# Message passing as matrix products: the order of high and low parts within a block of sources

## The chip, the cores and the metric

The kernel runs on one core of a Trainium2 chip. The metric is the device time of one execution in microseconds. The kernel before takes 4105.4 us, the median of three runs (4103.71 to 4105.85).

## The reference, cut to what matters

A graph of 6250 nodes with 128 features and 100,000 edges goes through four graph networks with a layer norm and a residual around each. Every layer sums, for each node, rows of its neighbours:

```python
agg = jax.ops.segment_sum(h[src], dst, num_segments=N)
```

This sum is needed three times in the first network (GIN: two dense layers with batch norm follow each time), once in the second (with a sigmoid gate per edge, then a GRU cell), five times in the third (a matrix product before the sum, a GRU cell after it) and once in the fourth (one matrix product after it). The edges are the same in all of them.

## The kernel before, in words

The kernel first sorts the edges and builds a matrix of counts: for each pair of nodes, how many edges go from the one to the other, one byte each, kept in DRAM. Nodes are padded to 49 blocks of 128 (`NB = 49`). A segment sum is then a dense product of the features with the count matrix. Counts are small integers; features are float32.

TensorE's one-pass float32 format (fp32r) does not keep all bits of a float32. So each 128x128 block of features is split in two: `high` (VectorE, L2540, the upper bits), copied to `hi` by ScalarE (L2402), and `lo`, the rest, by GpSimd (L2127). Both are multiplied with the same counts and added up in the same PSUM bank. This pair of products is L2188, the line of the change.

The targets are cut into three thirds (`THIRDS`), since PSUM holds only a part of all sums. For one third, TensorE goes through all 49 blocks of sources (`k` = 0 to 48) and adds each block's products up in four or five banks. These are the chunks of `SUMS`: third 0 has five chunks (384, 512, 512, 512, 512 columns), third 1 four of 512, third 2 four (512, 512, 512, 256). A block of sources of one third is called a source here; it is numbered `g` over the whole flow, and `g // 49` tells the part, a layer and a third of it. `k == 0` starts each bank anew, `k == NB - 1` ends it and tells the engines that take the sums out (`summed`, and `used` for the last chunk).

For each source, a DMA on SyncE's queue (L2073) brings a row of counts as bytes into a ring. ScalarE widens the first 1024 or 768 columns to fp32r (`wide_act`), VectorE the rest (`wide_dve`), both at L2036. There are three slots for widened rows and for `hi` and `lo`; `used`, which goes up with the last matmul of a source, frees them. Before a source's first matmul TensorE waits for `hi`, `lo` and `wide_act`; before the first chunk that goes beyond ScalarE's columns it waits for `wide_dve`.

The order of work on TensorE is written out by a loop over steps `g` (L2151). After each source it issues whatever of the layer behind is due at that step: products of the GRU cell (L2306 to L2309), dense layers (L2314, L2323), transposes (L2350) and others, each a few short matmuls in F32. `LAG`, `EVERY`, `LEAVE`, `ENTER` and `CHAIN` hold the distances in steps. There are two flows: the first with the three sums of the first network (one third of the first is made earlier, at L643) and the gated sum, the second with the five of the third network and the last one. The gated sum does not go by L2188: its counts are weighed by gates first (`weighing`), and its products are L2184, chunk after chunk with the same stationary block in plain F32. All others, 26 parts of 49 sources, go by L2188: nine of third 0, eight of third 1, nine of third 2.

Of the kernel before, what the change touches and what calls it, by code (L numbers as in the profile page):

```python
# [25 lines left out]
NB = -(-N // P)  # L26
# [32 lines left out]
SUMS = [[(128, 384), (512, 512), (1024, 512), (1536, 512), (2048, 512)],  # L59
        [(0, 512), (512, 512), (1024, 512), (1536, 512)],  # L60
        [(0, 512), (512, 512), (1024, 512), (1536, 256)]]
# [4 lines left out]
WIDE_SLOTS = 3  # L66
CUT_SLOTS = 3
# [1802 lines left out]
class Flow:  # L1870
# [95 lines left out]
    def run(self):  # L1966
        net, nc, ps = self.net, self.net.nc, self.net.ps
# [16 lines left out]
        with ExitStack() as tmp, stage(nc, *names) as (block, s):  # L1984
            wide = scratch(nc, tmp, "wide", [P, WIDE_SLOTS, ROW_BYTES], F32R)
            high = scratch(nc, tmp, "high", [P, CUT_SLOTS, P], I32)
            hi = scratch(nc, tmp, "hi", [P, CUT_SLOTS, P], F32R)
            lo = scratch(nc, tmp, "lo", [P, CUT_SLOTS, P], F32R)
# [11 lines left out]
            if self.enter is not None:  # L2000
                c0, size = row_slots * ROW_BYTES, self.enter.steps * 3 * D * 4
# [32 lines left out]
            def widen(copy, g, c0, c1):  # L2034
# [4 lines left out]
            whole, rest = (final[0:FULL_P * NB, :].rearrange("(p k) f -> p (k f)", k=NB),  # L2039
                           final[FULL_P * NB:N, :].rearrange("(a k) f -> a (k f)", a=1)) if final is not None else (None, None)  # L2040
# [105 lines left out]
            def _(e):  # L2146
                if self.enter is not None:
                    for n in range(self.enter.steps):
                        ins = e.transpose(ps[:, 2 + n // 4, n % 4 * D:(n % 4 + 1) * D], self.enter.weights[:, n, :], net.ident[:, :])
                    ins.then_inc(s["w_turned"], 1)  # L2150
                for g in self.steps:  # L2151
                    for n in combined_at(g):
                        e.wait_ge(s["w_cut"], 2)
                        for i in range(3):
                            ins = e.matmul(ps[:, n, i * D:(i + 1) * D], turned_w[:, n * D:(n + 1) * D], self.enter.w_in[i], start=True, stop=True)  # L2155
                        ins.then_inc(s["w_made"], 1)
                    if 0 <= g < total:
                        n, q, k = self.where(g)
                        weighing = g >= plain
                        if weighing:  # L2160
                            e.wait_ge(s["lv_sent"], self.need[n][k])
                        else:
                            e.wait_ge(s["hi"], g + 1)
                            e.wait_ge(s["lo"], g + 1)
                            e.wait_ge(s["wide_act"], g + 1)
                        early = not weighing
                        for c, (w0, size) in enumerate(SUMS[q]):
                            if early and w0 + size > BY_ACT[q]:
                                e.wait_ge(s["wide_dve"], g + 1)
                                early = False  # L2170
                            if weighing:
                                e.wait_ge(s["weighed"], self.weighed_upto(g, c))
                            if weighing and k == 0 and c == 4:
                                e.wait_ge(s["lv_relu"], len(leaves))
                                e.wait_ge(s["lv_scored"], len(leaves))
                            if self.enter is not None and g == 0:
                                e.wait_ge(s["w_kept"], self.enter.steps)
                            if k == 0 and g:
                                dve, act = self.taken(g // NB - 1, c + 1)
                                e.wait_ge(s["took_dve"], dve)  # L2180
                                if act:
                                    e.wait_ge(s["took_act"], act)
                            if weighing:
                                ins = e.matmul(ps[:, c, 0:size], source(n, k), weights(g, c), start=k == 0, stop=k == NB - 1,  # L2184
                                               skip_group_check=True)
                                ins.then_inc(s["attended"], 1)
                            for part in () if weighing else (hi, lo):
                                ins = e.matmul(ps[:, c, 0:size], part[:, g % CUT_SLOTS, :], wide[:, g % WIDE_SLOTS, w0:w0 + size],  # L2188
                                               start=k == 0 and part is hi, stop=k == NB - 1 and part is lo,
                                               skip_group_check=True)  # L2190
                            if not weighing and k == NB - 1 and c + 1 < len(SUMS[q]):
                                ins.then_inc(s["summed"], 1)
                        if not weighing:
                            ins.then_inc(s["used"], 1)

                    for c in self.entering_at(g - ENTER["turned"]):
# [5 lines left out]
                        for b in range(c.blocks):  # L2202
                            ins = e.transpose(ps[:, 5, b * P:(b + 1) * P], room[0][c.made % 2][:, b * P:(b + 1) * P], net.ident[:, :])  # L2203
                        ins.then_inc(s["turned"], 1)
                    for c in self.entering_at(g - ENTER["back"]):
# [4 lines left out]
                        for b in range(c.blocks):  # L2210
                            ins = e.transpose(ps[:, 5, PAIR + b * P:PAIR + (b + 1) * P], room[1][c.made % 2][:, b * P:(b + 1) * P],  # L2211
                                              net.ident[:, :])
# [36 lines left out]
                    for c in self.due(g - LEAVE["turned"], "leave"):  # L2249
# [5 lines left out]
                        for b in range(c.blocks):  # L2255
                            ins = e.transpose(ps[:, 6, b * P:(b + 1) * P], room[2][c.late % 2][:, b * P:(b + 1) * P], net.ident[:, :])
# [598 lines left out]
```

## Time and profile before

| | |
|---|---|
| median of three runs | 4105.4 us |
| span of the profiled execution | 4103.4 us |
| TensorE matmuls busy | 3757.5 us, 92% |
| TensorE weight loads busy | 2938.1 us, 72% |
| VectorE / ScalarE / GpSimd busy | 75% / 61% / 33% |
| matmuls at L2188 | 11074 |
| share of L2188 in the chain that ended last | 40% of the span |

The profile is of one execution; its span runs from the first instruction to the last, and no other time of that execution is given. PE is TensorE's matmuls, PEld its weight loads, DVE VectorE, ACT ScalarE, POOL GpSimd, SP SyncE. Matmuls overlap, so the duration of one is not what it costs; the distance between two starts in the timeline is. Starts are shown to 0.01 us.

### The profile page before, as it was taken

Reading aid. Unit: us, or ns where it says so; the run is one execution under the profiler, and the core shown is the slowest. Engines: PE = TensorE matmul, PEld = TensorE weight load, DVE = VectorE, ACT = ScalarE, POOL = GpSimd, SP = SyncE. Lnnn points to the kernel's source line nnn. Section 1 sums busy time; section 2 is a strip of 40 time slices with the busy share of each in tenths; the row PEclk is TensorE's granted clock in tenths of the full one; section 3 lists DMA queues with packets and bytes.
Section 4 is the critical chain, followed back from the end, with each engine's and each line's share of the span. In section 5 each row is a group of like instructions: output and inputs, shape, how many; then the busy total and the mean of one; then the engine's idle time right before and its main releaser. Section 6 shows DMA issues by size and latency. Waiting matters only on the chain.

```text
span 4103.4 us, 59929 instructions
## 1 busy us (share of the span) xinstructions
PE 3757.5 (92%) x17331; PEld 2938.1 (72%) x17331; DVE 3059.9 (75%) x5526; ACT 2493.7 (61%) x4754; POOL 1354.9 (33%) x1941
## 2 busy tenths in 40 slices
PE   0128899999999999999899999999999999999999
PEld 0116678888888644555688888888888888888887
DVE  9989956576587777878668667766866876786685
ACT  1119956656656787777565655565565565566655
POOL 0021135533545310000361343244244234346624
PEclk9999999999999999999999999999999999999999
DMA  2019964544543322221143344344344434433444
GB/s 63 0 56 363 366 197 124 141 130 124 144 130 105 93 70 77 71 63 54 58 113 108 107 128 119 107 126 125 108 121 123 110 104 129 121 100 110 117 133 135
DMA packets 234209, 489.81 MB, mean 119 GB/s; under 512 B 32580, under 2 KB 100925, under 8 KB 233496
## 3 DMA queue, kind: packets, MB, share of 16 engines
q1 hardware_dynamic: 213084, 432.93, 37.0%
q0 software_dynamic: 7856, 46.93, 3.2%
q10 hardware_dynamic: 12938, 6.05, 0.7%
q8 instruction: 146, 2.39, 0.3%
q14 instruction: 185, 1.51, 0.1%
HBM read 396.99 MB, written 43.87 MB: 107 GB/s over the span
## 4 chain that ended last, share of the span: by engine, by line
PE 50%; issue 0%; ACT 0%; DVE 0%; POOL 0%; ACTq 0%; POOLq 0%
PE ps L2188 40%; PE ps L2306 3%; PE ps L2307 3%; PE ps L2308 1%; PE ps L2309 1%; PE ps L2350 1%; PE ps L2336 0%; PE ps L2220 0%; PE ps L2292 0%; PE ps L2331 0%; PE ps L2226 0%; PE ps L2211 0%; ACT wide L2036 0%; PE ps L2203 0%; PE ps L2155 0%
## 5 line engine op out<-in xcount | busy, mean ns | idle before, releaser
L2188 PE MATMUL ps<-wide,hi 128*128 128x512 f32 (+2 forms) x5537 | 2135.8, 388 | 19.1 <-issue 9.5
L2188 PE MATMUL ps<-wide,lo 128*128 128x512 f32 (+2 forms) x5537 | 2075.4, 379 | 0.0
L2036 DVE CAST wide<-ring 128x1536 fp32r<-128x1536 uint8 (+2 forms) x1274 | 1311.7, 1030 | 551.0 <-PE ps L2188 546.5
L2188 PEld LDWEIGHTS ps<-wide,hi 128*128 128x128 f32 x5537 | 1041.1, 188 | 221.3 <-issue 29.5
L2188 PEld LDWEIGHTS ps<-wide,lo 128*128 128x128 f32 x5537 | 1042.8, 188 | 185.7
L2036 ACT CAST wide<-ring 128x768 fp32r<-128x768 uint8 (+1 forms) x1274 | 1153.0, 905 | 3.2 <-DMA ring<-count 2.3
L2402 ACT CAST hi<-high 128x128 fp32r<-128x128 f32 x1274 | 381.6, 299 | 983.8 <-PE ps L2188 605.2
L2127 POOL TENSOR_TENSOR lo<-hN,high 128x128 fp32r<-128x128 f32 x686 | 566.6, 829 | 761.5 <-PE ps L2188 468.5
L2127 POOL TENSOR_TENSOR lo<-hB,high 128x128 fp32r<-128x128 f32 x588 | 500.4, 852 | 763.2 <-PE ps L2188 545.6
L2184 PE MATMUL ps<-hN,hB 128*128 128x512 f32 (+1 forms) x1274 | 525.1, 569 | 5.6 <-DVE aggT L2365 4.2
L2395 ACT ACTIVATE hN<-aggT,source_scores 128x512 f32<-128x512 f32 (+1 forms) x637 | 428.7, 695 | 118.0 <-PE ps L2184 86.7
L2531 DVE TENSOR_TENSOR hN<-hN,ring 128x512 f32<-128x512 f32 (+1 forms) x637 | 402.8, 668 | 108.8 <-ACT hN L2395 103.7
L2184 PEld LDWEIGHTS ps<-hN,hB 128*128 128x128 f32 x1274 | 241.1, 191 | 263.5 <-issue 208.8
L2556 DVE SCALAR_TENSOR_TENSOR room<-ps,b2h,room 128x256 f32<-128x256 f32 (+1 forms) x125 | 59.8, 479 | 245.4 <-ACT room L2423 245.4
L2540 DVE TENSOR_SCALAR high<-hN 128x128 int32<-128x128 int32 x686 | 234.7, 342 | 8.9 <-DVE hB L2648 4.2
L2540 DVE TENSOR_SCALAR high<-hB 128x128 int32<-128x128 int32 x588 | 204.6, 348 | 0.6 <-POOL lo L2127 0.6
L679 ACT ACTIVATE aggT<-ps 128x1024 uint16<-128x1024 f32 x196 | 165.6, 846 | 26.3 <-PE ps L629 26.2
L475 PE MATMUL ps<-ident,aggT 128*128 128x128 f32 x112 | 27.6, 427 | 166.3 <-DVE aggT L184 166.3
L2423 ACT ACTIVATE room<-ps,b2s 128x256 f32<-128x256 f32 (+1 forms) x250 | 103.9, 467 | 119.7 <-PE ps L2309 118.6
L2307 PE MATMUL ps<-hT,wT 128*128 128x256 f32 (+1 forms) x600 | 175.8, 375 | 0.0
L629 PEld LDWEIGHTS ps<-right,left 128*128 128x128 bf16 x1225 | 99.2, 158 | 97.5 <-DVE left L586 46.7
L2090 POOL TENSOR_SCALAR states_bn<-states_bn 128x1 f32<-128x1 f32 x1 | 0.2, 231 | 506.6 <-POOLq L144 506.6
(246 smaller groups left out, 3477.1 us busy)
## 6 DMA issues: line engine op xcount, KB each, us to landing
ring<-count SPq DMA_DIRECT2D x490, 320.0 KB, 2.9
ring<-count SPq DMA_DIRECT2D x441, 256.0 KB, 2.6
ring<-count SPq DMA_DIRECT2D x490, 224.0 KB, 2.5
wide<-aggT POOLq DMA_DIRECT2D x49, 896.0 KB, 6.1
count<-aggT SPq DMA_DIRECT2D x49, 800.0 KB, 4.0
xN<-in_x ACTq DMA_DIRECT2D x1, 2744.0 KB
out<-xN SPq DMA_DIRECT2D x1, 1064.0 KB
out<-xN SPq DMA_DIRECT2D x1, 896.0 KB
```

Of the source, the lines that this page charges most:

```text
L679: e.activation(rows[k % ROW_BUFFERS][:, t0 * P:t1 * P], ps[:, bank:bank + 2, :].rearrange("p b f -> p (b f)") [:, 0:(t1 - t0) * P], ACT.Co ...
L2036: return copy(wide[:, g % WIDE_SLOTS, c0:c1].rearrange("p (t u f) -> p t u f", u=2, f=P), rows[:, g % row_slots, c0:c1].rearrange("p (t f ...
L2127: e.tensor_tensor(lo[:, g % CUT_SLOTS, :], source(n, k), high[:, g % CUT_SLOTS, :].bitcast(F32), ALU.subtract)\
L2184: ins = e.matmul(ps[:, c, 0:size], source(n, k), weights(g, c), start=k == 0, stop=k == NB - 1, skip_group_check=True)
L2188: ins = e.matmul(ps[:, c, 0:size], part[:, g % CUT_SLOTS, :], wide[:, g % WIDE_SLOTS, w0:w0 + size], start=k == 0 and part is hi, stop=k = ...
L2306: e.matmul(o, gates_of(c)[g_], net.aggT[:, c.cols], start=True, stop=False)
L2307: e.matmul(o, gru.w_state[g_], net.hT[:, c.cols], start=False, stop=True)
L2395: e.activation(weights(g, c), layers[n].target_scores[:, sums_at(q, c)], ACT.Sigmoid, bias=layers[n].source_scores[:, k:k + 1]).then_inc(s ...
L2402: e.copy(hi[:, g % CUT_SLOTS, :], high[:, g % CUT_SLOTS, :].bitcast(F32)).then_inc(s["hi"], 1)
L2423: e.activation(room[i][u][:, 0:c.size], ps[:, bank, i * PAIR:i * PAIR + c.size], ACT.Sigmoid, bias=self.step(c).b_sum[i]).then_inc(s["rz"], 1)
L2531: e.tensor_tensor(gate, gate, rows[:, g % row_slots, c0:c1].rearrange("p (t f u) -> p t u f", u=2, f=P), ALU.mult).then_inc(s["weighed"], 1)
L2540: e.tensor_scalar(high[:, g % CUT_SLOTS, :], source(n, k).bitcast(I32), HIGH_BITS, None, ALU.bitwise_and)\
```

## The change

For the sources `0 < k < NB - 1` of the parts that aren't weighed, the loop over the chunks issues only the product with `hi`; a second loop over the chunks then issues the products with `lo`. Before, each chunk got `hi` and then `lo`. The waits keep their place ahead of the chunks of the first loop, and `used` goes up with the last matmul of the second. The first and the last source of each part keep the old order, as do the products at L643 and L2184.

```diff
--- before.py
+++ after.py
@@ -2164,6 +2164,7 @@
                             e.wait_ge(s["lo"], g + 1)
                             e.wait_ge(s["wide_act"], g + 1)
                         early = not weighing
+                        whole = not weighing and 0 < k < NB - 1
                         for c, (w0, size) in enumerate(SUMS[q]):
                             if early and w0 + size > BY_ACT[q]:
                                 e.wait_ge(s["wide_dve"], g + 1)
@@ -2184,12 +2185,15 @@
                                 ins = e.matmul(ps[:, c, 0:size], source(n, k), weights(g, c), start=k == 0, stop=k == NB - 1,
                                                skip_group_check=True)
                                 ins.then_inc(s["attended"], 1)
-                            for part in () if weighing else (hi, lo):
+                            for part in () if weighing else (hi,) if whole else (hi, lo):
                                 ins = e.matmul(ps[:, c, 0:size], part[:, g % CUT_SLOTS, :], wide[:, g % WIDE_SLOTS, w0:w0 + size],
                                                start=k == 0 and part is hi, stop=k == NB - 1 and part is lo,
                                                skip_group_check=True)
                             if not weighing and k == NB - 1 and c + 1 < len(SUMS[q]):
                                 ins.then_inc(s["summed"], 1)
+                        for c, (w0, size) in enumerate(SUMS[q]) if whole else ():
+                            ins = e.matmul(ps[:, c, 0:size], lo[:, g % CUT_SLOTS, :], wide[:, g % WIDE_SLOTS, w0:w0 + size],
+                                           start=False, stop=False, skip_group_check=True)
                         if not weighing:
                             ins.then_inc(s["used"], 1)
 
```

## Rows read from the trace of the kernel before

**Rows 1.** The page: its first line, TensorE's busy time, and its granted clock in 40 slices.

```profile
span 4103.4 us, 59929 instructions
...
PE 3757.5 (92%) x17331; PEld 2938.1 (72%) x17331; DVE 3059.9 (75%) x5526; ACT 2493.7 (61%) x4754; POOL 1354.9 (33%) x1941
...
PEclk9999999999999999999999999999999999999999
```

**Rows 2.** The page, chain that ended last, shares of the span by line.

```profile
PE ps L2188 40%; PE ps L2306 3%; PE ps L2307 3%; PE ps L2308 1%; PE ps L2309 1%; PE ps L2350 1%; PE ps L2336 0%; PE ps L2220 0%; PE ps L2292 0%; PE ps L2331 0%; PE ps L2226 0%; PE ps L2211 0%; ACT wide L2036 0%; PE ps L2203 0%; PE ps L2155 0%
```

**Rows 3.** Groups of instructions: form, count, busy us, mean ns, idle before.

```profile
L2188 PE MATMUL ps<-wide,hi 128*128 128x512 f32 (+2 forms) x5537 | 2135.8, 388 | 19.1 <-issue 9.5 <-ACT wide L2036 5.7 <-ACT aggT L2367 1.5
L2188 PE MATMUL ps<-wide,lo 128*128 128x512 f32 (+2 forms) x5537 | 2075.4, 379 | 0.0
...
L2188 PEld LDWEIGHTS ps<-wide,lo 128*128 128x128 f32 x5537 | 1042.8, 188 | 185.7
...
L2184 PE MATMUL ps<-hN,hB 128*128 128x512 f32 (+1 forms) x1274 | 525.1, 569 | 5.6 <-DVE aggT L2365 4.2 <-DVE aggT L2369 1.4
...
L2184 PEld LDWEIGHTS ps<-hN,hB 128*128 128x128 f32 x1274 | 241.1, 191 | 263.5 <-issue 208.8 <-DVE hN L2531 38.3
```

**Rows 4.** One stretch: us, busy (x instructions) by engine, clock, DMA share, GB/s.

```profile
2400.00:2900.00 500.00, 499.43 (x2340) 421.37 (x2339) 355.65 (x603) 291.20 (x566) 184.54 (x209) 1.00 0.43 118
```

**Rows 5.** Line L2036 alone: who waited for it (us, times).

```profile
  PE ps L2188: 5.7, 1
```

**Rows 6.** Timeline at 1176 us: start, duration, engine, line, operation; VectorE, then TensorE.

```profile
1174.32 1.48 DVE L2036 CAST wide<-ring 128x1280 fp32r<-128x1280 uint8 x1
...
1176.59 0.40 PE L2188 MATMUL ps<-wide,lo 128*128 128x512 f32 x1
```

**Rows 7.** Timeline of TensorE, third 1; 16 matmuls of L2188 between these.

```profile
2582.73 0.39 PE L2188 MATMUL ps<-wide,hi 128*128 128x512 f32 x1
...
2586.58 0.39 PE L2188 MATMUL ps<-wide,lo 128*128 128x512 f32 x1
```

**Rows 8.** Timeline of TensorE, third 0, one source to the next.

```profile
2423.06 0.34 PE L2188 MATMUL ps<-wide,lo 128*128 128x384 f32 x1
2423.24 0.40 PE L2188 MATMUL ps<-wide,hi 128*128 128x512 f32 x1
...
2424.39 0.39 PE L2188 MATMUL ps<-wide,lo 128*128 128x512 f32 x1
...
2425.24 0.34 PE L2188 MATMUL ps<-wide,lo 128*128 128x384 f32 x1
```

**Rows 9.** Timeline of TensorE, third 2; the last row is eight sources later.

```profile
2707.14 0.28 PE L2188 MATMUL ps<-wide,lo 128*128 128x256 f32 x1
2707.26 0.40 PE L2188 MATMUL ps<-wide,hi 128*128 128x512 f32 x1
...
2720.10 0.28 PE L2188 MATMUL ps<-wide,lo 128*128 128x256 f32 x1
```

**Rows 10.** Timeline of TensorE, third 1, after two transposes; ten steps.

```profile
2589.40 0.38 PE L2350 MATMUL ps<-ident,hT 128*128 128x128 f32 x2
...
2589.85 0.39 PE L2188 MATMUL ps<-wide,lo 128*128 128x512 f32 x1
...
2592.16 0.39 PE L2188 MATMUL ps<-wide,lo 128*128 128x512 f32 x1
```

**Rows 11.** Timeline of TensorE, third 1, after one transpose; eight steps.

```profile
3209.70 0.27 PE L2350 MATMUL ps<-ident,hT 128*128 128x128 f32 x1
...
3210.05 0.39 PE L2188 MATMUL ps<-wide,lo 128*128 128x512 f32 x1
...
3211.87 0.39 PE L2188 MATMUL ps<-wide,lo 128*128 128x512 f32 x1
```

**Rows 12.** Timeline of TensorE: F32 passes, first and sixth row (x2: two passes).

```profile
2427.25 0.59 PE L2306 MATMUL ps<-aggT,ring 128*128 128x256 f32 x2
...
2429.41 0.59 PE L2309 MATMUL ps<-aggT,ring 128*128 128x256 f32 x2
```

## The prediction

> **What bounds the kernel now.** I read the page first. TensorE is busy for 3757.5 of 4103.4 us at the full granted clock, 2.4 GHz [rows 1], and the chain that ended last gives 40% of the span to L2188 alone [rows 2]. In a 500 us window of the second flow PE is busy for 499.43 us at clock 1.00 [rows 4]: here the time is what TensorE needs to get through its list. The groups of instructions [rows 3] then give the list: L2188 issues 5537 matmuls with the high part and as many with the low part, 11074 in all, and next to them just as many weight loads. The sum of the parts agrees: nine parts of third 0, eight of third 1 and nine of third 2, each with 49 sources at 10, 8 and 8 matmuls, are 4410 + 3136 + 3528 = 11074.
>
> The mean of 388 ns in that group is a latency, not a price, because matmuls overlap. The price is the distance from start to start in the timeline. In a quiet stretch of third 1, where all chunks have 512 columns, 17 starts take 2586.58 - 2582.73 = 3.85 us, 0.2265 us each [rows 7]. Within this stretch half of the steps go from the high to the low part of one chunk (same bank, same moving data, other weights) and half from the low part to the next chunk's high part (everything changes), and the pace does not tell them apart.
>
> **What the change touches.** For 47 of 49 sources of each part (k = 0 and k = 48 stay) 11074 x 47/49 = 10622 matmuls are put in another order. None is added or removed. No instruction of another engine moves. The sum goes part by part:
>
> 1. Weight loads. After the change 4 of 5 (third 0) or 3 of 4 matmuls use the weights that the one before used. Does their load go away? The kernel has the same situation in L2184, where all chunks of a source are multiplied with one stationary block in a row: 637 products there are 1274 matmul passes with 1274 loads [rows 3]. So repeated weights are loaded again. These are F32 products of two passes each, so they don't prove it for the one-pass format of L2188, but they are the nearest rows. I take 11074 loads before and after. A load takes 188 ns and a matmul step 226.5, and PE's idle time before all of L2188's matmuls is 19.1 us, next to nothing of it for a load [rows 3]: loads lie under the matmul before. Kept or dropped, I cost them at 0; the end below zero, a stream that runs faster under unchanged weights, is rival C.
>
> 2. The wait for VectorE's half of the widened row. It now comes before the third matmul of a source instead of the fifth (third 0), and before the second instead of the third elsewhere: 0.45 or 0.23 us earlier. Queued behind it on PE is the whole rest of the source. In the whole trace PE waited for a widening once, for 5.7 us [rows 5], and the groups name ScalarE's half for it [rows 3]. The tightest place I found is at 1176 us: VectorE's cast starts at 1174.32 and takes 1.48, so it ends at 1175.80; the second matmul of that source, which will have the wait in front of it, starts at 1176.59 [rows 6]. That leaves 0.79 us. Cost 0; if this cover were gone, each source would lose at most the 0.23 or 0.45 us by which the wait is earlier, and none of them comes near.
>
> 3. Release of buffers and banks. The count that frees the widened row and the weight buffers still goes up with the last matmul of the source. Take-outs of the banks hang on k = 48, which keeps its order. The low part has been waited for at the source's start, as now. Cost 0.
>
> 4. The order of long and short matmuls. This is the only part for which the trace shows a price. A source of third 1 has equal chunks. A source of third 2 has 3584 columns over both parts, at 0.2265 us per 512 that is 1.585 us; eight sources in a row take 2720.10 - 2707.14 = 12.96 us, 1.620 each [rows 9]. So 35 ns are lost per source. Third 0 has 4864 columns, 2.152 us, and takes 2425.24 - 2423.06 = 2.18 [rows 8]: 28 ns lost. In third 1 nothing is lost, though the same conversions run beside it. What is different is the short chunk: 256 or 384 columns, twice in a row (high, low), after which the following 512s start 0.23 to 0.24 apart for a while (five steps from 2423.24 take 1.15 us, 1.132 at the steady pace) [rows 8]. Today these stretches cost 441 x (0.035 + 0.028) = 27.8 us, of which 423 x 0.063 = 26.6 lie in the reordered sources. After the change the two short matmuls of a source no longer stand together: each has three or four long ones behind it. So the cost lies between all of it gone (-26.6 us) and doubled (+26.6 us).
>
> To choose between the ends I looked at other short matmuls. After two 128-column transposes the ten steps from 2589.85 take 2.31 us, 45 ns over the steady 2.265 [rows 10]; after a single one the eight steps from 3210.05 take 1.82, 8 ns over 1.812 [rows 11]. That speaks for singles being cheaper than half a pair. Against it: within a pair the second short matmul is already late in giving way: 0.18 instead of 0.170 us for 384 columns [rows 8], 0.12 instead of 0.113 for 256 [rows 9]. So one short matmul before it is enough to start the loss, and after the change there would be two starts per source. I take the middle, 0. It is what one gets if the loss goes with the number of short matmuls, which doesn't change.
>
> Sum: 0 + 0 + 0 + 0 on 4103.4 us of span, which stands 2.0 us under the median of the runs, 4105.4. Forecast 4105 us.
>
> **Against a page.** The trace has one load per matmul, hidden, at 188 ns under a step of 226.5 [rows 3, 7]. The Trainium skill, "TensorE: Matmul & The Clock Gate", section "Step-by-step: what each phase is for", says that weights usually stay in the array over many matmuls, so that they are loaded once and used repeatedly; by that rule this order would be the better one. The same page under "Back-to-back issue gap" gives 512/2.4 + 2.5 = 216 ns for a 512-column step; the trace has 226.5 and the measurement decides. By the page the sum would gain some 10 ns on each step with unchanged weights, by the rows nothing.
>
> **Rivals.**
>
> A, slower: each short chunk restarts the slow stretch. The place is the step after each 256 or 384 column matmul of L2188. Full doubling is 26.6 us; in third 2 only three long matmuls follow a short one where six do now, so a stretch is cut in half, and third 0 sources near a gated chunk start in one anyway. Half the doubling, +13 us: 4118. It decides when a single short matmul is followed by more than half of today's loss.
>
> B, faster: a lone short matmul costs little, as after the lone transpose. Two singles are 16 of the 45 ns of a pair, so 64% of 26.6 us goes: -17 us, 4088. The two transposes are F32 and follow F32 products, which is what speaks against carrying their numbers over.
>
> C, faster by much: with unchanged weights the stream itself speeds up. What speaks for it: the nearest matmuls of about the same length, 256-column F32 passes, come every 2.16/10 = 0.216 us [rows 12], so 0.2265 is no floor. Of the 10622 matmuls, 423 x 8 + 376 x 6 + 423 x 6 = 8178 follow one with the same weights; at up to 10.5 ns that is 86 us: 4020. Against it: in those F32 passes the weights change each time, and the pace is as good, so weights are not what makes L2188 slower.
>
> D, slower: a step to another bank with the same weights, or the earlier wait, costs something that no row shows, 1 to 2 ns per matmul, 10 to 20 us: 4120.
>
> **How the numbers follow.** About 8 us, 0.2%, is what a measurement of this kernel can tell from no change. That is 0.8 ns per reordered matmul, so the middle is narrow. The forecast gets 0.45, with 4098 to 4112 as its own range: 0.39 of it within 0.2%, 0.03 on each side. A gets 0.24, B 0.20, C 0.07, D 0.04. Faster: 0.03 + 0.20 + 0.07 = 0.30. Same: 0.39. Slower: 0.03 + 0.24 + 0.04 = 0.31. The range from 4087 to 4121 holds the forecast, A, B and most of D, and leaves out C.
>
> **What would show it.** The page after should have 11074 loads at L2188 again; fewer would make step 1 wrong. A quiet stretch of third 1 should keep its 0.2265 us per matmul; if it gets shorter, C is right, if longer, D. The period of a third 2 source (1.620) and of a third 0 source (2.18) decide between the forecast, A and B: 20 to 30 ns up is A, as much down is B. A new wait of PE for VectorE's L2036 would make step 2 wrong. My prediction is wrong if the period of any of the three kinds moves by more than 15 ns.

## The result and the profile after

The changed kernel takes 4112.45 us (median of 16 runs, 4109.90 to 4113.42). The kernel before, run in turn with it on the same chip, takes 4104.97 us (16 runs, 4102.96 to 4106.57). The ratio is 1.0017, 95% interval 1.0010 to 1.0024: slower by 7.5 us. That is a hair under the 8 us that the prediction set as the bound of "no change", but the interval of this comparison leaves no change out, and 4112.45 lies above the forecast's own range of 4098 to 4112 and inside the wide one. The mechanism was forecast at zero, and it is not zero.

The page after: first line, busy times, granted clock, and the chain by line. It answers to [rows 1, 2].

```profile
span 4111.7 us, 59929 instructions
...
PE 3766.1 (92%) x17331; PEld 2938.1 (71%) x17331; DVE 3060.2 (74%) x5526; ACT 2493.8 (61%) x4754; POOL 1353.0 (33%) x1941
...
PEclk9999999999999999999999999999999999999999
...
PE ps L2189 21%; PE ps L2195 19%; PE ps L2310 3%; PE ps L2311 3%; PE ps L2313 1%; PE ps L2312 1%; PE ps L2354 1%; PE ps L2340 0%; PE ps L2224 0%; PE ps L2296 0%; PE ps L2335 0%; PE ps L2230 0%; PE ps L2215 0%; ACT wide L2036 0%; PE ps L2207 0%
```

This profiled execution took 4113.42 us, span 4111.7: 8.3 us over the span of before. The same 17331 matmuls and as many loads are there, PE is busy 8.6 us longer, and VectorE and ScalarE do what they did. L2188 has become L2189 (all high parts, and both parts at k = 0 and 48) and L2195 (the low parts); their shares of the chain, 21 and 19%, are the 40% of before. The time is in PE's stream itself. The two lines by form, as in [rows 3], and, from line L2036 alone, who waited for it, as in [rows 5]:

```profile
L2189 PE MATMUL ps<-wide,hi 128*128 128x512 f32 (+2 forms) x5537 | 1490.1, 389 | 19.0 <-issue 9.5 <-ACT wide L2036 5.7 <-ACT aggT L2371 1.5
L2195 PE MATMUL ps<-wide,lo 128*128 128x512 f32 (+2 forms) x5311 | 1348.5, 379 | 0.0
...
L2189 PEld LDWEIGHTS ps<-wide,hi 128*128 128x128 f32 x5537 | 995.6, 188 | 210.9 <-issue 29.6 <-DVE aggT L2369 2.6 <-ACT hi L2406 1.8
L2195 PEld LDWEIGHTS ps<-wide,lo 128*128 128x128 f32 x5311 | 961.0, 188 | 189.7
...
L2189 PEld LDWEIGHTS ps<-wide,lo 128*128 128x128 f32 x226 | 43.2, 191 | 6.9
```

```profile
  PE ps L2189: 5.7, 1
```

5537 + 5311 + 226 = 11074 loads, as before: repeated weights are loaded again. Idle time ahead of the matmuls stays at 19.0 us, and the one wait for a widening is still the 5.7 us one. (The busy column can't be held against before: matmuls of one line that follow each other overlap, and now four or five do, so the overlaps count once.)

**Where the time is.** First the steady pace. In the timeline x4 or x5 means that many matmuls in one row. After, TensorE in a quiet stretch of third 1, two sources and a half, up to the products of the GRU cell:

```profile
2586.28 1.07 PE L2195 MATMUL ps<-wide,lo 128*128 128x512 f32 x4
2587.18 1.07 PE L2189 MATMUL ps<-wide,hi 128*128 128x512 f32 x4
...
2589.90 1.07 PE L2195 MATMUL ps<-wide,lo 128*128 128x512 f32 x4
2590.81 0.59 PE L2310 MATMUL ps<-aggT,ring 128*128 128x256 f32 x2
```

20 steps take 4.53 us, 0.2265 each, exactly [rows 7]. Then the starts of four parts in a row, after and before: third 0, third 1, third 2, the next third 0.

```profile
2726.54 0.41 PE L2189 MATMUL ps<-wide,hi 128*128 128x384 f32 x1 [0.30 <-ACT aggT L2371]
...
2854.01 0.47 PE L2189 MATMUL ps<-wide,hi 128*128 128x512 f32 x1
...
2970.12 0.47 PE L2189 MATMUL ps<-wide,hi 128*128 128x512 f32 x1
...
3072.58 0.41 PE L2189 MATMUL ps<-wide,hi 128*128 128x384 f32 x1 [0.30 <-ACT aggT L2371]
```

```profile
2722.30 0.41 PE L2188 MATMUL ps<-wide,hi 128*128 128x384 f32 x1 [0.30 <-ACT aggT L2367]
...
2849.33 0.47 PE L2188 MATMUL ps<-wide,hi 128*128 128x512 f32 x1
...
2965.43 0.47 PE L2188 MATMUL ps<-wide,hi 128*128 128x512 f32 x1
...
3067.76 0.41 PE L2188 MATMUL ps<-wide,hi 128*128 128x384 f32 x1 [0.30 <-ACT aggT L2367]
```

Third 0 goes from 127.03 to 127.47 us, +0.44; third 1 from 116.10 to 116.11; third 2 from 102.33 to 102.46, +0.13. Over 47 sources that is 9 ns a source in third 0 and 3 in third 2 (other third 2 parts have +0.21: 4 to 5). A part's length is read to 0.01 us, a source's only to 10 ns, so the part is the better ruler. By it I took the difference of all 26 parts. All columns are in us against the profile of before. The last three are runs described below: after_again, third0_only and before_later4.

```
                                  after  same kernel  third 0  order of
                                         again        alone    before, 4 products ahead
third 0, first part               +0.67     +0.18      -0.05     -1.71
third 0, the other eight          +2.78     +2.93      +2.82     +0.09
third 1, all eight                +0.13     +0.18      +0.16     +0.16
third 2, seven parts              +1.03     +1.18      -0.05      0.00
third 2, gated part (1280-2020)   +1.79     +1.33      +1.32     +1.48
third 2, part with 3771           +1.73     +0.14      +1.49     -0.02
```

Two things are in this table. The order itself costs some 2.9 us in the eight later parts of third 0 and 1.1 in seven parts of third 2; the four traces of the changed kernel, as it is or with a few products added, agree within 0.3 us. And three single parts, the first and the last two of the table, move from trace to trace by up to 2 us, in kernels that have the old order there too. Those three are mainly the clock. Two windows, around the start of the gated sum and around 3771 us (us, busy by engine, granted clock, DMA share, GB/s), before and after:

```profile
1380.00:1400.00 20.00, 15.77 (x43) 8.22 (x42) 15.99 (x26) 15.97 (x25) 0.00 (x0) 0.91 0.27 68
3760.00:3790.00 30.00, 27.74 (x133) 23.23 (x133) 19.12 (x37) 18.22 (x35) 18.24 (x25) 1.00 0.52 144
```

```profile
1380.00:1400.00 20.00, 15.76 (x45) 8.69 (x44) 14.59 (x24) 14.85 (x22) 0.68 (x1) 0.83 0.28 80
3760.00:3790.00 30.00, 26.53 (x123) 21.62 (x122) 18.37 (x38) 18.35 (x37) 20.58 (x34) 0.94 0.50 136
```

The clock has two levels here, 2.4 and 1.2 GHz, and a stretch at 1.2 GHz counts half. So a mean of 0.91 over 20 us is about 3.6 us at half speed, 0.83 is 6.8 us, and 0.94 over 30 us is 3.6 us; half of each is lost. Before each stands an idle time of TensorE that both kernels have. The one ahead of the gated sum, before:

```profile
1387.16 5.23 PE L2184 MATMUL ps<-hN,hB 128*128 128x512 f32 x8 [4.24 <-DVE aggT L2365]
```

It is 4.24 us after the change too. The one ahead of 3771, before and after:

```profile
3767.27 0.47 PE L2188 MATMUL ps<-wide,hi 128*128 128x512 f32 x1 [1.96 <-issue]
```

```profile
3773.38 1.51 PE L2189 MATMUL ps<-wide,hi 128*128 128x512 f32 x4 [1.96 <-issue]
```

The idle time is 1.96 us in both, and only after is the clock halved behind it: four matmuls take 1.51 us where they take 1.07 elsewhere. None of this was in the prediction.

The third place is the start of the first flow. The clock is at half there in both kernels when the first part begins, and for how much longer differs from trace to trace. The first 10 us of that part in before, after, third1_only (old order in this part) and before_later4:

```profile
542.83:552.83 10.00, 10.00 (x37) 8.42 (x38) 5.88 (x9) 6.03 (x11) 5.34 (x5) 0.78 0.98 346
```

```profile
542.84:552.84 10.00, 10.00 (x35) 8.32 (x36) 5.35 (x9) 5.59 (x10) 4.81 (x5) 0.73 0.91 330
```

```profile
542.28:552.28 10.00, 10.00 (x35) 8.38 (x35) 5.25 (x9) 5.48 (x10) 4.06 (x5) 0.72 0.94 338
```

```profile
548.67:558.67 10.00, 10.00 (x46) 8.33 (x45) 4.09 (x6) 4.68 (x8) 3.72 (x3) 1.00 0.56 194
```

That is 2.2, 2.7, 2.8 and 0 us lost. It accounts for +0.5 of the +0.67 after, for the +0.52 of third1_only (which starts this part 0.55 us earlier, so that nothing is lost in all), and for the -1.71 in the last column of the table, whose first part begins behind the half clock. The order itself is left with about +0.2 in the first part.

The runs without a profile can't be sorted by what happened at 3771. The nine of the 16 with a mean clock of 0.993 or 0.994 have a median of 4112.8 us, the seven with 0.995 one of 4110.5, but the mean adds up all the falls of an execution. The profile of after_later1 (below) has the fall at 3771 and a mean of 0.995.

### The profile page after: what moved, and what is told of

Read it like the earlier page. It is cut to its first block, busy times and chain, and to the rows that moved or that the text cites. A ratio compares the mean times of both kernels' runs of the same rounds, so it can differ in the third digit from the quotient of the medians.

```text
span 4111.7 us, 59929 instructions
## 1 busy us (share of the span) xinstructions
PE 3766.1 (92%) x17331; PEld 2938.1 (71%) x17331; DVE 3060.2 (74%) x5526; ACT 2493.8 (61%) x4754; POOL 1353.0 (33%) x1941
## 4 chain that ended last, share of the span: by engine, by line
PE 50%; issue 0%; ACT 0%; DVE 0%; POOL 0%; ACTq 0%; POOLq 0%
PE ps L2189 21%; PE ps L2195 19%; PE ps L2310 3%; PE ps L2311 3%; PE ps L2313 1%; PE ps L2312 1%; PE ps L2354 1%; PE ps L2340 0%; PE ps L2224 0%; PE ps L2296 0%; PE ps L2335 0%; PE ps L2230 0%; PE ps L2215 0%; ACT wide L2036 0%; PE ps L2207 0%
## 5 line engine op out<-in xcount | busy, mean ns | idle before, releaser
L2036 DVE CAST wide<-ring 128x1536 fp32r<-128x1536 uint8 (+2 forms) x1274 | 1312.1, 1030 | 556.7 <-PE ps L2195 542.4
L2189 PE MATMUL ps<-wide,hi 128*128 128x512 f32 (+2 forms) x5537 | 1490.1, 389 | 19.0 <-issue 9.5
L2195 PE MATMUL ps<-wide,lo 128*128 128x512 f32 (+2 forms) x5311 | 1348.5, 379 | 0.0
L2036 ACT CAST wide<-ring 128x768 fp32r<-128x768 uint8 (+1 forms) x1274 | 1153.2, 905 | 3.2 <-DMA ring<-count 2.3
L2189 PEld LDWEIGHTS ps<-wide,hi 128*128 128x128 f32 x5537 | 995.6, 188 | 210.9 <-issue 29.6
L2195 PEld LDWEIGHTS ps<-wide,lo 128*128 128x128 f32 x5311 | 961.0, 188 | 189.7
L679 ACT ACTIVATE aggT<-ps 128x1024 uint16<-128x1024 f32 x196 | 165.6, 846 | 26.6 <-PE ps L629 26.5
```

What stands on the lines that cost most here:

```text
L679: e.activation(rows[k % ROW_BUFFERS][:, t0 * P:t1 * P], ps[:, bank:bank + 2, :].rearrange("p b f -> p (b f)") [:, 0:(t1 - t0) * P], ACT.Co ...
L2036: return copy(wide[:, g % WIDE_SLOTS, c0:c1].rearrange("p (t u f) -> p t u f", u=2, f=P), rows[:, g % row_slots, c0:c1].rearrange("p (t f ...
L2195: ins = e.matmul(ps[:, c, 0:size], lo[:, g % CUT_SLOTS, :], wide[:, g % WIDE_SLOTS, w0:w0 + size], start=False, stop=False, skip_group_che ...
```

## The experiments

Each kernel ran on a chip together with the kernel before, and its ratio is to that. The medians of before: 4105.42 for third1_only, shorts_together and the two equal ones; 4104.87 for third0_only, mirror, four_shorts and before_later; 4105.48 for before_later6, before_later4, after_later1 and after_again; 4105.71 for the two filled ones. A ratio of 11 runs carries an interval of about 0.0009, or 3.7 us, to each side, so kernels 1 to 2 us apart are told apart by the parts of their profiles and not by these medians. "Quiet part" means a part of third 0 and of third 2 in the stretch of the rows above, in the second flow (127.03 and 102.33 us before).

**third1_only: the new order only where all chunks are equal.** It has the repeated weights, the steps to another bank and the earlier wait, without short chunks.

```
-  whole = not weighing and 0 < k < NB - 1
+  whole = not weighing and 0 < k < NB - 1 and q == 1
```

> The new order only in third 1, where all chunks have 512 columns. Theory (slow stretches after short chunks): the matmul step stays 0.2265 us, the eight third 1 parts take the same 860.3 us from their second to their last source, time within 1 us of the kernel before. Rival (the weights that stay, the change of bank or the earlier wait for VectorE cost something per matmul): third 1 gets longer by its share of the change, some 2 to 3 of the 7.5 us. Second rival (half-clock spells come more often in the new order, wherever it is): more than 3.4 us of spells beyond those of the kernel before.

4105.39 against 4105.42 us, ratio 0.9999 [0.9990, 1.0008]; the eight third 1 parts together +0.03 us. So repeated weights gain nothing, and the other bank and the earlier wait cost nothing there: rivals C and D fall. The Trainium skill, "TensorE: Matmul & The Clock Gate", section "Step-by-step: what each phase is for", has weights loaded once and used repeatedly; here this order has the load each time and no gain, and the measurement decides.

**third0_only: the counterpart.** The same line with `and q == 0`.

> The new order only in third 0. From the trace of the changed kernel, third 0 as a whole is 3.5 us longer and third 2 1.0 us without its two clock spells. Theory: this kernel takes 3.5 us more than before plus what clock spells it gets, 4109. Rival (all of the change comes from clock spells): 4105 to 4107, with third 0 as before.

4110.39 us, 1.0013 [1.0004, 1.0022]. The starts of third 0, third 1, third 2 and the next third 0 in it:

```profile
2725.10 0.41 PE L2189 MATMUL ps<-wide,hi 128*128 128x384 f32 x1 [0.30 <-ACT aggT L2371]
...
2852.55 0.47 PE L2189 MATMUL ps<-wide,hi 128*128 128x512 f32 x1
...
2968.66 0.47 PE L2189 MATMUL ps<-wide,hi 128*128 128x512 f32 x1
...
3070.97 0.41 PE L2189 MATMUL ps<-wide,hi 128*128 128x384 f32 x1 [0.30 <-ACT aggT L2371]
```

127.45 us (+0.42), 116.11, and 102.31, the old value. The loss of the quiet parts sits where the order is new. But its part with the gap at 3771 is longer by 1.49, with the old order in it and a mean clock of 0.94 in the same window as above: that part of the loss is not the order of that part's matmuls.

**shorts_together: the new order, third 0's short chunk last with the high part and first with the low part.** The two 384s of a source stand together again.

```
+  chunks = list(enumerate(SUMS[q]))
+  if whole and q == 0: chunks = chunks[1:] + chunks[:1]
   ... high part over chunks, low part over reversed(chunks)
```

> The new order, but each source's high loop ends with its short chunk and the low loop begins with it and goes through the chunks backwards, so that the two short matmuls stand together again, and weights still stay for 4 or 3 of the matmuls in a row. Theory: third 0 back to 2.18 us per source, third 2 to 1.62, total 4.5 us below the changed kernel (half-clock spells aside). Rival (unchanged weights or order of banks cost): as slow as the changed kernel, +0.17%.

4111.38 us, 1.0014 [1.0005, 1.0023]: 6.0 us over before, where I had expected some 3. The sequence of lengths is now exactly that of before (two shorts, then eight or six 512s), and only weights and banks follow each other differently. Starts of third 0 and third 1:

```profile
2726.90 0.41 PE L2192 MATMUL ps<-wide,hi 128*128 128x384 f32 x1 [0.32 <-ACT aggT L2374]
...
2854.06 0.47 PE L2192 MATMUL ps<-wide,hi 128*128 128x512 f32 x1
```

127.16 us, +0.13 where the new order has +0.44. In third 2 the reversal brings the two 256s together as well, and its quiet parts stay at +0.14 to +0.18, no less than after. So in the quiet parts splitting the pair costs 0.3 us of 0.44 in third 0 (7 ns a source) and nothing in third 2; the rest, 3 to 4 ns a source in both, is there with unchanged lengths. In the first flow the pair gains nothing: two parts of third 0 keep +0.28 to +0.30, as in after, and two parts of third 2 have +0.33, more than the +0.17 and +0.08 of after. Over the same eight and seven parts as in the table above the two thirds lose 1.9 and 1.3 us where after loses 2.8 and 1.0, so keeping the pairs together gives back some 0.6 of 3.8 us. Most of the loss is there although the lengths follow each other as before. It needs the short chunk all the same, since third1_only has none and costs nothing. The first part has +0.77, and both stretches of half clock are there (gated part +1.47, the part with 3771 +1.53).

**equal_before and equal_after: no short chunks at all**, third 0 as 4 x 486 + 488, third 2 as 4 x 448 columns, in the old and the new order.

```
+  PLAIN_SUMS = [[(128, 486), (614, 486), (1100, 486), (1586, 486), (2072, 488)],
+                SUMS[1], [(448 * c, 448) for c in range(4)]]
```

> The order of before, but the chunks of thirds 0 and 2 are of (nearly) one size: 486, 486, 486, 486, 488 and 4 x 448 columns instead of 384 + 4 x 512 and 3 x 512 + 256. Theory: no short chunk, no slow stretch: 2.152 us per source in third 0 instead of 2.180, 1.585 instead of 1.620 in third 2, 27 us less in all if 486 columns stream as well per column as 512: 4078 us. Rival (the loss belongs to the thirds' other work, not to the sizes): 4105 us.

> The same equal chunks with the new order. Theory: without short chunks the order costs nothing, so the same time as equal chunks in the old order, within 2 us. Rival (weights, banks or the wait): 7 us slower than that.

4117.80 us, 1.0029 [1.0018, 1.0041], and 4116.01 us, 1.0029 [1.0018, 1.0039]. The old order should have gained 27 us if short chunks were the whole cost. Its timeline, 14 steps of 448 columns:

```profile
2727.89 0.37 PE L2191 MATMUL ps<-wide,lo 128*128 128x448 f32 x1
...
2730.78 0.37 PE L2191 MATMUL ps<-wide,lo 128*128 128x448 f32 x1
```

2.89 / 14 = 0.206 us a step, where 448/512 of 0.2265 is 0.198. My 28 and 35 ns of "loss" per source were not only the price of a change of length: these sizes miss the steady pace even among themselves. (The chunks of 486 columns in third 0 also begin at other places of the widened row, which these two kernels don't separate from the size.) What the pair does settle is the order: with no shorts the new order is not slower than the old (a quiet third 0 part +0.78 against +1.13, third 2 +0.44 against +0.49 in most). The new order costs only where lengths differ.

**mirror: the old order, odd sources with their chunks backwards.** Four shorts meet, and there are half as many changes of length.

```
+  if not weighing and 0 < k < NB - 1 and k % 2:
+      chunks = chunks[::-1]
```

> The high and low products chunk by chunk as before, but every second source of a part goes through its chunks backwards, so that the short matmuls of two neighbouring sources stand four in a row and then 12 or 16 long ones. Theory 'per start' (each run of short matmuls costs one slow stretch, however many they are): the loss of 28 and 35 ns per source halves, 13 us less, 4092 us. Rival 'per short matmul' (the forecast's assumption): 4105 us, no change. Rival 'an order that differs costs by itself': above 4107.

4108.55 us, 1.0008 [0.9999, 1.0018]. The timeline where two shorts meet two:

```profile
2744.98 0.33 PE L2191 MATMUL ps<-wide,hi 128*128 128x384 f32 x1
2745.15 0.34 PE L2191 MATMUL ps<-wide,lo 128*128 128x384 f32 x1
2745.33 0.34 PE L2191 MATMUL ps<-wide,hi 128*128 128x384 f32 x1
2745.51 0.35 PE L2191 MATMUL ps<-wide,lo 128*128 128x384 f32 x1
2745.69 0.40 PE L2191 MATMUL ps<-wide,hi 128*128 128x512 f32 x1
```

Four shorts take 0.71 us, 0.68 at the steady pace. The quiet parts gain 0.12 (third 0) and 0.17 us (third 2), 3 to 4 ns a source, where a price per change of length gives 14 to 17 and a price per short matmul gives 0. So a fifth of the loss goes with the changes, and the rest is as good as untouched by halving them. Its part around 3771 is longer by 4.04 us: an idle time 18 us ahead of the gap grew from 1.41 to 2.61 us, and the clock fell there and behind the gap.

**four_shorts: the old order, two shorts instead of one** (448, 448, 512, 512, 512 and 512, 512, 384, 384), by the same table PLAIN_SUMS.

> The order of before with other chunk sizes: 448, 448, 512, 512, 512 in third 0 and 512, 512, 384, 384 in third 2, which makes four shorter matmuls in a row in each source. Theory 'per start': the loss per source stays about 28 and 35 ns, 4105 us. Rival 'per short matmul': it doubles, 4130 us. Rival 'sizes' (each chunk that isn't 512 columns costs by its own size, 448 some 5 ns over its share as with equal chunks): third 0 loses 20 ns from its four 448s and little else, 4100 to 4108.

4114.96 us, 1.0025 [1.0015, 1.0036], which is none of the three times expected; quiet parts +0.91 and +0.40, which is 19 and 9 ns a source, with as many changes of length as before: again neither 0 nor the doubling (28 and 35). But by equal_before a step of 448 among its like costs 8 ns over its share, so this number can't be divided further, and the kernel tells little.

**before_later, before_later6, before_later4: the old order, pushed later** by 7, 6 or 4 more F32 products of 512 columns ahead of the first source, to see whether the place in time alone brings the half clock.

```
+  if self.enter is None and g == 0:
+      for _ in range(DELAY):
+          e.matmul(ps[:, 0, 0:512], net.ident[:, :], net.hT[:, 0:512], start=True, stop=True)
```

> The kernel before, with seven extra F32 products of 512 columns (never read) ahead of the first source of the first flow, which move everything behind them about 6 us later. Theory 'place decides' (the changed kernel gets a half-clock spell at 3773 us because it arrives 6 us later at TensorE's idle gap of 2 us there): this kernel gets that spell too, in about as many runs as the changed one (granted clock 0.993 in half of them), and those are some 2 us above the rest: median 4112. Rival 'the order causes the spells': no spell, 4111 us in all runs, with clock 0.994 to 0.996.

> The kernel before with six extra F32 products ahead instead of seven, so everything behind comes 5.3 us later instead of 6.2. Theory 'position' (TensorE's 1.95 us gap near 3770 us is followed by a half-clock spell or not depending on where exactly it falls; 6.2 us later was a lucky place, 5.3 is not): this kernel gets the spell in most runs, granted clock 0.993 to 0.994, and is as slow as with seven products or slower although it is delayed less: 4111 to 4113. Rival 'the order of the products brings the spells on': no spell in the old order at any delay, 4110.3, clock 0.994 to 0.996.

> The same with four extra products, 3.6 us later. Theory 'position': no spell at the gap, as in the kernel before, 4108.5 us, clock 0.994 to 0.996. Rival 'any delay brings it': 4110.3 and clock 0.993.

4111.58, 4110.74 and 4108.99 us; 1.0017 [1.0008, 1.0026], 1.0013 [1.0004, 1.0022], 1.0009 [1.0000, 1.0018]. None has the half clock at 3771, though I had expected it of before_later and then of before_later6. before_later, with its gap ending 0.06 us from the place where it ends after the change:

```profile
3773.44 0.47 PE L2192 MATMUL ps<-wide,hi 128*128 128x512 f32 x1 [1.96 <-issue]
```

```profile
3760.00:3790.00 30.00, 26.54 (x130) 22.02 (x129) 19.15 (x40) 18.97 (x38) 21.23 (x34) 1.00 0.53 145
```

So "that place on the time axis" fell as the cause in its simple form. At the gated part they do tell something. before_later4 and before_later, the window 1380 to 1400:

```profile
1380.00:1400.00 20.00, 15.77 (x51) 9.71 (x50) 14.21 (x24) 14.44 (x23) 1.97 (x3) 0.83 0.31 90
```

```profile
1380.00:1400.00 20.00, 15.77 (x57) 10.27 (x56) 14.79 (x25) 15.04 (x24) 2.88 (x4) 0.91 0.38 103
```

The first has 0.83 and its gated part is longer by 1.48 us, the second 0.91 and +0.24: both have the order of before, so the order isn't needed for this difference. Over all traces, those with 0.91 have -0.08 to +0.71 us in this part and those with 0.83 have +1.10 to +2.20, with one exception (mirror: 0.83 and +0.54).

**after_later1 and after_again: the changed kernel with one such product, and unchanged once more.**

> The changed kernel with one extra F32 product of 512 columns ahead, 0.9 us more work. Theory 'position': most of its runs lose the spell, the group with clock 0.993 shrinks from half of the runs to a quarter or less, and the median falls or stays in spite of the extra work: 4111.4. Rival 'the order brings the spells on': 4113.3, half of the runs at 0.993.

> The changed kernel as it is, on the same chip as the three others, to compare with. All theories: 4112.4 us, two groups of runs, at 4110.5 and 4112.8; if the profiled run is one without the spell at 3773 us, its span is 1.7 us shorter than that of the first profile.

4111.22 us, 1.0014 [1.0005, 1.0023], and 4112.56 us (4109.54 to 4114.87), 1.0017 [1.0008, 1.0026]. The kernel with more work has the lower median, by 1.3 us, and 2 of 11 runs with a mean clock of 0.993 or less instead of 6 of 11; the intervals overlap. Its profile doesn't bear out that it avoids the fall at 3771: the fall is there (that part +1.72), and it is the longer half clock at the gated part that is missing (+0.50). The profile of after_again caught the changed kernel without the half clock at 3771:

```profile
3760.00:3790.00 30.00, 26.52 (x129) 21.80 (x128) 19.12 (x39) 19.08 (x38) 21.25 (x35) 1.00 0.52 143
```

Span 4109.5 instead of 4111.7, the part with 3771 at +0.14 instead of +1.73, all quiet parts of third 0 again +0.43 or +0.44. The half clock comes and goes between executions of one kernel; the loss from the order doesn't.

**after_filled and before_filled: five F32 products of 128 columns put into the gap at 3771**, in both kernels.

```
+  if self.enter is not None and g == FILL_AT:      # step 728
+      for _ in range(5):
+          e.matmul(ps[:, 4, 0:P], net.ident[:, :], net.ident[:, :], start=True, stop=True)
```

> The changed kernel with five extra 128-column F32 products (never read) on TensorE just ahead of the source whose first matmul comes after the 1.95 us gap at 3771 us; they run inside that gap and shorten it to about 0.9 us. Theory (in half of the runs and more, the changed kernel loses some 2 us to a half-clock spell that this gap sets off, besides the 4.3 us of its matmul order): no run at clock 0.993 or below on account of it, the upper group of runs goes, median 4110.6 instead of 4112.5, third 2 of the last GRU layer 0.1 us over that of the kernel before. Rival (the two groups of runs have another cause): two groups as before, median 4112.5.

> The kernel before with the same five products in the same gap, as a control. Theory: it had no spell there, so nothing changes, 4105.4 us. Rival (the extra products cost or gain something by themselves): off by more than 1 us.

4111.56 us, 1.0014 [1.0005, 1.0023], and 4105.24 us, 0.9999 [0.9990, 1.0008]. The gap shrank:

```profile
3774.23 1.04 PE L2193 MATMUL ps<-wide,hi 128*128 128x512 f32 x4 [0.84 <-issue]
```

The four matmuls behind it take 1.04 us again and the part is at +0.21 us. But after_again has no fall there either with its gap unfilled, so one profile can't show that the filling prevents it. The median moved less than I expected, to +5.9 us over before instead of +7.5 (+7.1 in after_again), and the upper runs did not go: five of 11 lie above 4112 us. None of the 11 has a mean clock of 0.993 or less, which adds up all falls. Taken at its face the median puts 1.2 to 1.6 us on the half clock at 3771, which agrees with the 1.6 us between the two profiles of the changed kernel, but the intervals of these medians overlap, and this is not shown by them.

## Why the prediction was wrong

**The account**, in us, for the profiled execution, which is 8.3 over that of before. Order: 2.8 in the eight parts of third 0, about 0.2 in the first, 1.0 in third 2, together 4.0. Clock: 0.5 in the first part, 1.8 in the gated part, 1.7 at 3771, together 4.0. Third 1 and what stands behind the last part add 0.2. So half of the loss is the order and half the clock.

For the median of many runs the first half holds, since every profile of the changed kernel has it, and the second is an estimate. With the order of before in the gated part, three traces with 0.83 have +1.30 there on the mean and three with 0.91 have +0.11, so the longer half clock costs about 1.2; with the new order four have +1.67 and one +0.50. With 1.2 to 1.6 for 3771 the sum is 6.4 to 6.8 of the 7.1 to 7.5 measured. The first part moves with the clock too: by -0.5 to +0.8 us against before in the traces that start it within 1.2 us of the same time.

**Step 1, weight loads: right.** 11074 loads again, 0 us, and third1_only shows that it is 0 on the clock too. C at 4020 is out.

**Step 2, the earlier wait, and step 3, releases: right.** PE's only wait for L2036 is the old one of 5.7 us, and VectorE's busy time is unchanged. D is out as it was put, on every reordered matmul; 3 to 4 ns a source that could be of its kind are left in the quiet parts of thirds 0 and 2, and no run separates the bank, the weights and the wait there.

**Step 4, the order of long and short matmuls: the step that failed.** It was the only term that the prediction gave a price, and its size was set to 0, the middle between -26.6 and +26.6. It measured +4: 15% of the doubling (9 of 28 ns a source in third 0, 3 to 5 of 35 in third 2), rival A's direction at a third of its 13 us. The place was right: the loss stands only in the thirds with a short chunk. The mechanism was right in small part: step 4 put the whole question on the two shorts standing apart, and shorts_together, which puts them together again, gives back some 0.6 of 3.8 us. The reason for the middle, that the loss doesn't go with the changes of length, holds for most of it, as mirror shows from the other side: half the changes give back only a fifth of what they would if the loss went with them. That 0 came within 4 us, between ends of -26.6 and +26.6, is partly luck, since the middle was chosen and not worked out. The base was misread too: equal_before shows that 28 and 35 ns are not the price of a short chunk as against none, so a fraction of them could not be worked out from [rows 8, 9] in any case. And the lone transpose of [rows 11], B's ground, didn't carry over. The sign was in the text already: two starts of the slow stretch per source where there was one. I quoted it and then took zero, where a small plus was the reading. The sign of being wrong was too coarse as well: no period moved by the 15 ns that it asks for, and 9 ns times the 423 reordered sources of third 0 would be 3.8 us.

**The missing term: the clock.** I read the granted clock in 40 slices, all 9, and called it full; but a 9 only says 90% or more, of a slice of 103 us. Then I read one 500 us window, 1.00, and stopped. The trace of before has 0.91 in the window 1380 to 1400, behind 4.24 us of idle TensorE, and another idle time of 1.96 us without a fall, and the prediction names neither. A change that moves everything behind it by 1 to 6 us could be asked what it does at those two places, which measured up to 1.8 us each.

**Still open.** What decides whether the clock falls behind the same gap. It isn't the gap's length (1.96 us with and without), nor the order in that part (third0_only has the fall with the old order), nor the time since the start alone (3773.38 with, 3773.44 without). Seven profiles show a fall in the part around 3771: five with the new order in third 0 (after, third0_only, shorts_together, equal_after, after_later1) and two of the old order with other lengths or sequence (equal_before, mirror). None of the three that are only delayed does. A tie to the sequence of matmuls is therefore neither shown nor excluded, but the same kernel both with and without the fall (after, after_again) speaks against it.

One rival was not tested: the place of the gap against the clock's own changes in the same execution, which aren't tied to the program's start. The first fall around the start of the first flow begins at 534.50 us in after and at 533.49 in after_again. Counted from that fall, the gap at 3771 begins 3236.0 to 3237.0 us later in after, after_later1, third0_only and shorts_together, all four with the fall behind it, and 3237.4 to 3238.4 us later in after_again, before_later4 and before_later, all three without. The other traces lie further off on both sides, some with a fall and some without, so this gives no rule, and no run set that distance on purpose. But the second group holds the changed kernel as well as the order of before. Open too is why sources with a short chunk lose time when the same lengths come with other weights and banks, which is most of the order's 4 us, and by what rule lengths under 512 miss their columns.

## What to carry to other kernels

Before reordering matmuls of unequal length, measure what a mixed row of them costs beyond its columns, and don't take a price from matmuls of another kind. Don't count on repeated weights: separating high and low parts gained nothing from them and lost 9 ns a source in the quiet parts of third 0, 7 of them by splitting its pair of short ones. When a change moves a program by a few us, list TensorE's idle times and the granted clock behind each in windows of 20 to 30 us: 40 slices of a 4 ms program don't show 3.6 us at half clock, and three such places were here half of what one profile showed. Two profiles of the same kernel tell which part of a difference stays.

## What the runs showed of the hardware

The time of a one-pass matmul here doesn't go by its columns: among their like, 512 take 226.5 ns a step and 448 take 206 (198 by columns). The same weights in four or five matmuls in a row are loaded four or five times (11074 loads before and after), and for four in a row, in third1_only, at no cost and no gain (+0.03 us over eight parts).
